# Last product of a pair of experts: one float32 matmul per half tile, or three products of split halves with the weights' halves kept in a table

## What is computed

```python
scores = x @ expert_tokens.T                  # 8 experts, hidden size 64
_, topk_idx = top_k(scores, 2)
for i in range(8):
    w = mean(topk_idx == i)                   # 0.5 for the two chosen experts, else 0
    h = gelu(x @ W1[i] + b1[i])               # [.., 1024] x [1024, 64]
    h = gelu(h @ W2[i] + b2[i])               # [.., 64] x [64, 64]
    y = h @ W3[i] + b3[i]                     # [.., 64] x [64, 1024]
    outputs = outputs + y * w
x = x + outputs                               # x on the right was normalised again for the experts
```

## Time and profile before

| | |
|---|---|
| median of 3 runs | 1637.22 us (1632.99 to 1646.51) |
| the profiled execution | 1640.42 us, its span 1638.7 us |
| mean granted TensorE clock | 0.961 of full |
| busy: TensorE, VectorE, ScalarE, GpSimd | 1489.0, 1193.0, 687.0, 681.2 us |
| moved by DMA | 306.94 MB, 187 GB/s over the span |

### The profile page before, as it was taken

One profiled execution on the slowest core, in us unless ns is written; L12 is line 12 of the kernel. 1 busy time (PEld: TensorE's weight loads), 2 busy tenths in 40 slices (PEclk: granted clock), 3 DMA queues, 4 the chain that ended last, 5 costly groups with the idle time before them and its releaser, 6 DMA issues.

```text
span 1638.7 us, 28903 instructions
## 1 busy us (share of the span) xinstructions
PE 1489.0 (91%) x9321; PEld 1235.5 (75%) x9321; DVE 1193.0 (73%) x2415; ACT 687.0 (42%) x1365; POOL 681.2 (42%) x769
## 2 busy tenths in 40 slices
PE   6999999999699656998989957999999999999997
PEld 5999999999577335877767746777777777777775
DVE  5666666666388675898988974777777777777775
ACT  2444445454243630000000005666566566656653
POOL 2112222223675004677666543444444444444432
PEclk9999999999799887999999978999999999999999
DMA  8888875552564098799999757677677666765420
GB/s 204 227 179 193 174 199 152 163 140 67 133 207 119 1 266 201 208 293 287 264 255 286 211 151 220 211 220 224 213 217 217 208 206 207 218 207 157 120 56 15
DMA packets 121961, 306.94 MB, mean 187 GB/s; under 512 B 64155, under 2 KB 65857, under 8 KB 114315
## 3 DMA queue, kind: packets, MB, share of 16 engines
q1 hardware_dynamic: 60088, 155.40, 34.2%
q0 software_dynamic: 61728, 149.74, 32.6%
HBM read 220.40 MB, written 138.85 MB: 219 GB/s over the span
## 4 chain that ended last, share of the span: by engine, by line
PE 46%; issue 20%; DMA 11%; POOL 9%; DVE 8%; SPq 1%; POOLq 0%; DVEq 0%; ACT 0%
PE psum L1888 14%; DMA agg<-node_table,from_idx 8%; PE psum L1856 7%; PE psum L1564 7%; PE psum L1565 6%; PE psum L1566 6%; PE psum L1886 4%; DVE stat L967 2%; POOL where_from L606 2%; POOL agg L663 2%; DVE cx L1325 2%; POOL xls L639 1%; POOL td L643 1%; POOL rstd L595 1%; PE psum L1744 1%
## 5 line engine op out<-in xcount | busy, mean ns | idle before, releaser
L1888 PE MATMUL psum<-w_raw,gl 128*128 128x512 f32 x528 | 269.2, 591 | 0.0
L911 ACT ACTIVATE xt_hi<-psum 128x512 fp32r<-128x512 f32 x264 | 151.0, 597 | 238.4 <-PE psum L1856 238.3
L1492 DVE TENSOR_TENSOR xt_lo<-psum,xt_hi 128x512 fp32r<-128x512 f32 x264 | 176.3, 688 | 86.3 <-ACT xt_hi L911 86.2
L1603 PE MATMUL psum<-wdx_hi,axt_hi 128*125 128x272 f32 x640 | 191.4, 299 | 6.8 <-DVE wd_lo L1034 4.0
L1505 DVE SCALAR_TENSOR_TENSOR xb<-psum,xb 128x512 f32<-128x512 f32 x264 | 176.0, 686 | 28.0 <-PE psum L1888 27.7
L995 DVE TENSOR_TENSOR axt_lo<-psum,axt_hi 128x500 fp32r<-128x500 f32 x160 | 108.4, 678 | 118.8 <-ACT axt_hi L771 118.8
L1856 PEld LDWEIGHTS psum<-ident,xn 128*128 128x128 f32 x1056 | 126.4, 142 | 86.8 <-issue 68.3
L1605 PE MATMUL psum<-wdx_hi,axt_lo 128*125 128x272 f32 x640 | 185.5, 290 | 0.0
L1604 PE MATMUL psum<-wd_lo,axt_hi 128*125 128x256 f32 x640 | 180.2, 281 | 0.0
L743 POOL DMA_INDIRECT out<-xb,idx_in x132 | 133.8, 1014 | 106.1 <-issue 59.4
L905 ACT ACTIVATE xn<-xb 128x1024 f32<-128x1024 f32 x132 | 156.1, 1233 | 45.1 <-DMA xb<-rows_x,idx_in 45.1
(11 more groups left out here) (277 smaller groups left out, 3872.1 us busy)
## 6 DMA issues: line engine op xcount, KB each, us to landing
w_raw<-in_L_ffn_W SPq DMA_DIRECT2D x140, 256.0 KB, 12.7
cx<-in_x POOLq DMA_DIRECT2D x20, 1792.0 KB, 15.3
rows_x<-cx SPq DMA_DIRECT2D x19, 1806.0 KB
ax<-in_x SPq DMA_DIRECT2D x19, 1792.0 KB
node_table<-trow SPq DMA_DIRECT2D x19, 896.0 KB
node_table<-xld SPq DMA_DIRECT2D x10, 448.0 KB
cx<-in_x POOLq DMA_DIRECT2D x20, 208.0 KB, 23.1
rows_x<-cx SPq DMA_DIRECT2D x19, 209.6 KB
```

Source lines behind the costliest of these rows:

```text
L1492: dve.tensor_tensor(xt_lo[:, 2 * q:2 * q + 2, :].rearrange("p k n -> p (k n)"), T_R[q % 2], xt_hi[:, 2 * q:2 * q + 2, :].rearrange("p k n ...
L1603: pe.matmul(into, high, wdx_hi[:, k, :], start=k == 0, stop=False, skip_group_check=True)
L1888: pe.matmul(Y[u], gl2[:, t % 2, rows], w3_raw[:, t % N3, HALF * n:HALF * (n + 1)], start=False, stop=True, skip_group_check=True).then_inc ...
```

## The change

In the expert tiles `down` multiplies by halves. `gelu_2` is followed by a copy of its result to float32r (`gl2_hi`, ScalarE) and VectorE subtracts (`low_2`, between the next tile's `low_r` and the last two `result`s). The last product becomes three float32r matmuls of 512 columns, and its wait is for the low half instead of the gelu.

The weights' halves come from a new table in DRAM, `w3_parts`, with high and low half side by side in rows of 2,048 numbers. It is made during the projection: SyncE loads all of w3 (2 MB) at group 0, ScalarE and VectorE split a quarter of it in each of groups 2 to 5, and SyncE stores both parts (4 MB) at group 7. As the same room on chip then takes w1, w1's pieces move from groups 1 to 8 to groups 8 to 11, two a group, behind a wait for that store; `w_up` moves from group 9 to 12, and the splitting of w1 to groups 13 to 16, two pieces a group. `load_w3` now brings both halves of a tile's weights, 64 rows of 8 KB for either expert.

Some semaphores are merged to make room for the new ones (the one for the padding with `raw_small`, those for w_up's low halves and for the routing weights into `up_ready`, those for the staged w1 and w2 into `r_w`); the counts that are waited for follow.

```diff
         rows_x1 = nc.dram_tensor("rows_x1", [N, ROW], F32)
+        w3_parts = nc.dram_tensor("w3_parts", [NE * EH, 2 * D], F32)
         lists = nc.dram_tensor("lists", [(PAIRS + 1) * CAP, 1], I32)
...
         tok_rows = put("tok_rows", [NE, D], F32, at1 + 2 * KH * D * 4)
+        w3_low, w3_high, w3_end = run_of(
+            at1 + 2 * KH * D * 4, ("w3_low", [128, NE // 2, D], F32), ("w3_high", [128, NE // 2, D], F32R))
+        assert w3_end <= at2
         before_raw, ones_raw, rest_raw, bcap_i, p_i, b3_hi, b3_raw, late_end = run_of(
...
-        xb, xn0, w3_raw, st_w1, st_w2, r_end = run_of(
+        xb, xn0, w3_hl, st_w1, st_w2, r_end = run_of(
             at3,
-            ("xb", [128, NX, NS, ROW], F32), ("xn0", [128, D], F32), ("w3_raw", [128, N3, D], F32),
+            ("xb", [128, NX, NS, ROW], F32), ("xn0", [128, D], F32), ("w3_hl", [128, N3, 2, D], F32R),
             ("st_w1", [128, 2, 2, KD, 128], F32R), ("st_w2", [128, 2, 2, 128], F32R))
...
         ranks = RK[0:P, 0:J * PAIRS].rearrange("p (j b) -> p j b", j=J)
+        w3_e = w3_parts[:, :].rearrange("(e h) n -> e h n", h=EH)
         x1_g = rows_x1[:, :].rearrange("(g p j) d -> g p (j d)", p=P, j=J)
...
         WP0, WS0 = 0, 4
-        GW1, GS1 = 1, 11
+        GS3, GP3, GW1, GS1 = 2, 7, 8, 13
...
                     load_x(g + NAX)
-                if GW1 <= g < GW1 + KD:
-                    k = g - GW1
-                    sp.dma_start(w1_raw[:, :, 1, k, :],
-                                 w1[:, 128 * k:128 * (k + 1), :].rearrange("e p h -> p e h")).then_inc(raw_w1, 16)
-                if g == GW1 + KD:
+                if g == 0:
+                    sp.wait_ge(tok_tp, 1)
+                    sp.dma_start(w3_low[:, :, :], w3.rearrange("(q a) h n -> (a h) q n", a=2)).then_inc(raw_ffn, 16)
+                if g == GP3:
+                    sp.wait_ge(ffn_lo, NE // 2)
+                    for part, source in ((0, w3_high[:, :, :].bitcast(F32)), (1, w3_low[:, :, :])):
+                        sp.dma_start(w3_parts[:, D * part:D * (part + 1)].rearrange("(q p) n -> p q n", p=2 * EH),
+                                     source).then_inc(w3_put, 16)
+                if GW1 <= g < GW1 + KD // 2:
+                    sp.wait_ge(w3_put, 32)
+                    for k in (2 * (g - GW1), 2 * (g - GW1) + 1):
+                        sp.dma_start(w1_raw[:, :, 1, k, :],
+                                     w1[:, 128 * k:128 * (k + 1), :].rearrange("e p h -> p e h")).then_inc(raw_ffn, 16)
+                if g == GW1 + KD // 2:
                     sp.dma_start(wup_raw[:, :, :], w_up.rearrange("(k p) n -> p k n", p=128)).then_inc(raw_wup, 16)
...
                         wait(sp, w3_in, 32 * t)
-                    sp.dma_start(w3_raw[EH * a:EH * (a + 1), t % N3, :],
-                                 w3[bass.ds(slot + a, 1), :, :].rearrange("e h n -> (e h) n")).then_inc(w3_in, 16)
+                    sp.dma_start(w3_hl[EH * a:EH * (a + 1), t % N3, :, :].rearrange("p v n -> p (v n)").bitcast(F32),
+                                 w3_e[bass.ds(slot + a, 1), :, :].rearrange("e h n -> (e h) n")).then_inc(w3_in, 16)
...
+            def high_w3(q):
+                act.wait_ge(raw_ffn, 16)
+                act.activation(w3_high[:, q, :], w3_low[:, q, :], ACT.Copy).then_inc(ffn_hi, 1)
+
             def high_w1(k):
-                act.wait_ge(raw_w1, 16 * KD)
+                act.wait_ge(raw_ffn, 16 * (1 + KD))
                 hi, _, raw = w1_piece(k)
-                act.activation(hi, raw, ACT.Copy).then_inc(w1_hi, 1)
+                act.activation(hi, raw, ACT.Copy).then_inc(ffn_hi, 1)
...
                     empty_left(i - 1)
-                if i % J == 1 and 0 <= i // J - GS1 < KD:
-                    high_w1(i // J - GS1)
+                if i % J == 1 and 0 <= i // J - GS3 < NE // 2:
+                    high_w3(i // J - GS3)
+                if i % J in (1, 2) and 0 <= i // J - GS1 < KD // 2:
+                    high_w1(2 * (i // J - GS1) + i % J - 1)
                 if i == 0:
...
                 act.activation(gl2[:, t % 2, :], H2[:, 0:TT], ACT.Gelu, bias=b2_of(pair)).then_inc(r_g2, 1)
+                act.wait_ge(r_g2, t + 1)
+                act.activation(gl2_hi[:, t % 2, :], gl2[:, t % 2, :], ACT.Copy).then_inc(r_g2hi, 1)
...
+            def low_w3(q):
+                dve.wait_ge(ffn_hi, q + 1)
+                dve.tensor_tensor(w3_low[:, q, :], w3_low[:, q, :], w3_high[:, q, :].bitcast(F32), ALU.subtract
+                                  ).then_inc(ffn_lo, 1)
+
             def low_w1(k):
                 hi, lo, raw = w1_piece(k)
-                dve.wait_ge(w1_hi, k + 1)
+                dve.wait_ge(ffn_hi, NE // 2 + k + 1)
                 dve.tensor_tensor(lo, raw, hi.bitcast(F32), ALU.subtract)
...
                         late_setup(2 * j + 4)
-                if j == J - 1 and 0 <= g - GS1 < KD:
-                    low_w1(g - GS1)
+                if j == J - 1 and 0 <= g - GS3 < NE // 2:
+                    low_w3(g - GS3)
+                if j >= 2 and 0 <= g - GS1 < KD // 2:
+                    low_w1(2 * (g - GS1) + j - 2)
                 if i == J + 1:
...
+            def low_2(t):
+                dve.wait_ge(r_g2hi, t + 1)
+                dve.tensor_tensor(gl2_lo[:, t % 2, :], gl2[:, t % 2, :], gl2_hi[:, t % 2, :].bitcast(F32), ALU.subtract
+                                  ).then_inc(r_g2lo, 1)
+
             def first_of(t):
...
                     low_r(t + 1, 1)
+                low_2(t)
                 if t >= 1:
...
                 if q == 0:
-                    pe.wait_ge(r_w1, 2 * (t + 1))
+                    pe.wait_ge(r_w, 3 * t + 2)
                     wait(pe, r_g1, t)
...
                     pe.wait_ge(w3_in, 32 * (t + 1))
-                    pe.wait_ge(r_g2, t + 1)
+                    pe.wait_ge(r_g2lo, t + 1)
                 wait(pe, r_res, 4 * (t - 1) + u + 1)
-                rows = slice(128 * s, 128 * (s + 1))
+                rows, cols = slice(128 * s, 128 * (s + 1)), slice(HALF * n, HALF * (n + 1))
                 pe.matmul(Y[u], sel_st[:, t % 2, :], b3_hl[:, HALF * n:HALF * (n + 1)], start=True, stop=False,
                           skip_group_check=True)
-                pe.matmul(Y[u], gl2[:, t % 2, rows], w3_raw[:, t % N3, HALF * n:HALF * (n + 1)], start=False, stop=True,
-                          skip_group_check=True).then_inc(r_y, 1)
+                product(Y[u], (gl2_hi[:, t % 2, rows], gl2_lo[:, t % 2, rows]),
+                        (w3_hl[:, t % N3, 0, cols], w3_hl[:, t % N3, 1, cols]), False, True).then_inc(r_y, 1)
             turn_r(0, 1)
```

More of the change, by code:

```diff
@@ L140, in build @@
             ("steps", [P, J, PAIRS], F32), ("slot_f", [P, J], F32))
-        (gl1, h1_hi, h1_lo, gl2, sel_st, routed_end) = run_of(
+        (gl1, h1_hi, h1_lo, gl2, gl2_hi, gl2_lo, sel_st, routed_end) = run_of(
             0,
             ("gl1", [128, TT], F32), ("h1_hi", [128, TT], F32R), ("h1_lo", [128, TT], F32R),
-            ("gl2", [128, 2, TT], F32), ("sel_st", [128, 2, 128], F32R))
+            ("gl2", [128, 2, TT], F32), ("gl2_hi", [128, 2, TT], F32R), ("gl2_lo", [128, 2, TT], F32R),
+            ("sel_st", [128, 2, 128], F32R))
         xn1, xn_end = run_of(routed_end, ("xn1", [128, D], F32))
@@ L297, in build @@
         r_h2, r_g2, r_y, r_res = sem("r_h2"), sem("r_g2"), sem("r_y"), sem("r_res")
-        r_w1, r_w2, r_sel = sem("r_w1"), sem("r_w2"), sem("r_sel")
+        r_w, r_sel = sem("r_w"), sem("r_sel")
+        r_g2hi, r_g2lo = sem("r_g2hi"), sem("r_g2lo")
         w2_up, w3_in = sem("w2_up"), sem("w3_in")
@@ L629, in _ @@
             pool.wait_ge(setup_v, 9)
-            pool.wait_ge(pad_zero, 16)
+            pool.wait_ge(raw_small, 16 * 8)
             for b in range(NBG):
@@ L1105, in late_setup @@
                 elif k == 6:
-                    dve.wait_ge(b3_split, 1)
+                    dve.wait_ge(setup_v, 11)
                     dve.tensor_scalar(b3_raw[:, :], b3_raw[:, :], dup_rest[:, 0:1], None, ALU.mult
-                                      ).then_inc(b3_split, 1)
+                                      ).then_inc(setup_v, 1)
                 elif k == 7:
-                    dve.wait_ge(b3_split, 2)
+                    dve.wait_ge(setup_v, 12)
                     dve.scalar_tensor_tensor(b3_hl[0:2 * NE, :], b3_hi[:, :].bitcast(F32), dup_mask[:, 0:1],
@@ L1153, in routing_weights @@
                 product = M2[:, 0:KH * NE].rearrange("p (m e) -> p m e", m=KH)
-                dve.tensor_copy(m2[:, :, 0:NE], product).then_inc(m2_split, 1)
-                dve.wait_ge(m2_split, 1)
+                dve.tensor_copy(m2[:, :, 0:NE], product).then_inc(up_ready, 1)
+                dve.wait_ge(up_ready, WP0 + 5 - WS0 + 2)
                 dve.tensor_tensor(m2[:, :, NE:2 * NE], product, m2[:, :, 0:NE].bitcast(F32), ALU.subtract
-                                  ).then_inc(m2_split, 1)
+                                  ).then_inc(up_ready, 1)
             def low_d(c):
```

(4 more changed lines are left out.)

23 lines of the change are left out of this document (11 added, 12 removed).

## The result

The change made the kernel slower: 1672.06 us, the median of four runs (1663.90 to 1687.55), against 1635.11 us for the kernel before (four runs, 1631.67 to 1646.51). The ratio is 1.0203, with a 95% interval of 1.0158 to 1.0247. The forecast was 1601, with a range up to 1624. The profiled execution took 1669.48 us (span 1667.8), 29.1 more in span than the one of before.

What follows compares the result with a forecast made beforehand. TensorE was taken to bound tiles and projection. Terms -43 + 4 + 2 + 1 = -36 us took the profiled 1640.42 to 1604.4, and 3.2 less for the median gave 1601 us; range 1590 to 1624.

Steps and rivals of the forecast that it cites:

- Part 2: Expert tiles' doubled last-weight loads: no cost in loaded tiles (286 GB/s, share 0.93), 4 us at the stage's start.
- -43: Last product in the expert tiles: 0.163 us less a call, 0.65 a tile, 43 us in 264 calls.
- The DMA engines take over: Rival: DMA engines bound the loaded tiles at 274 GB/s, 9.28 us a tile, 1622 us in all; chance 0.15.
- Slower: Rival: DMA engines lose pace in the tiles; at 248 GB/s 10.24 us a tile, +38, 1675 us; chance 0.04.
- the share of 0.9 to 0.95: Sign in the tiles: the DMA engines' share, expected at this level if the forecast held.
- ScalarE's wait for gathered rows: Sign in the tiles: if ScalarE's normalisation waits for gathered rows, the DMA engines are the bound; forecast expected none.
- Tiles over 9.2 us: Sign that the prediction is wrong: expert tiles taking longer than this, where 8.90 us was forecast.
- low_2 and the copy hidden: In the tiles the new VectorE subtraction and ScalarE copy cost nothing, with 0.35 us a tile left on VectorE.
- The start: Start of the tiles: 1 MB more ahead of tile 0's upper w2 on SyncE's queue, taken as 4 us.
- The case of an 8 KB row as two packets: At the tiles' start: split rows would make both loads nearly twice as long beside gathers, up to 12 us more.
- The projection: Making the table in the projection: 2 us for four VectorE subtractions, 1 us for a late table store.
- The late table store: Projection, group 0: w3's 2 MB ahead of the store delays ScalarE's buffer by 0 to 4 us, taken as 1.

Runs made afterwards that it cites:

- e13: Changed kernel with four w3 loads of 32 rows a tile instead of two of 64, each to every other partition within its half: 1686.36 us.
- e14: Changed kernel with four w3 loads of 32 rows a tile instead of two of 64, each to every fourth of all partitions: 1621.50 us.
- e7: Changed kernel with each expert's w3 rows loaded to every other partition instead of one half (product pairs wrong rows): 1597.78 us.
- e2: Changed kernel with w3 loads counted on two semaphores in turn, so two tiles' w3 are in flight: 1685.39 us.
- e11: Changed kernel with the second expert's w3 load on ScalarE's queue, the first's staying on SyncE's: 1689.13 us.
- e15: Changed kernel with four w3 loads of 64 rows of 4 KB a tile, to every other partition (wrong rows): 1634.14 us.
- e1: Changed kernel loading only the high halves of w3 (512 KB a tile), used in place of the low halves too: 1607.09 us.
- e9: Changed kernel with both experts' hidden rows interleaved, so w3 loads to every other partition and the product stays right: 1604.79 us, 0.9773 of the kernel before.
- e10: e9 with w3 loaded behind group 0's table store, its table steps one group later, and tile 0's upper w2 ahead of w3: 1602.42 us, ratio 0.9753.
- e5: Kernel before with the product by halves, but no table: w3 loaded as before and divided in each tile by ScalarE and GpSimd: 1660.69 us.

## Why the prediction was wrong

- **The step that failed** is in Part 2, "Cost taken: nothing": "the engines manage 306 GB/s on this mix", and so 2.54 MB in 8.90 us at a share of 0.93. The added bytes aren't of the mix. They are loads to half the partitions, which take the engines at 229 GB/s (e13 237, against e14's 317). By the row of before that was left unread (243) the added 0.52 MB would have taken 2.2 us of all engines, beside 0.69 x 9.56 = 6.6: 8.8 of 8.90 us, no room left. Measured are 0.94 x 10.01 = 9.4, so 256 / 0.94 = 272 GB/s for a full share in place of 306; with spread loads (e7) it is 276 / 0.84 = 329. In the 0.6 us of a tile that are left the engines aren't all busy; e2 and e11, with more in flight, come to a share of 0.95, and what holds the rest back (SyncE's order, as in e15, or something else) no run separates. The loaded tile became 10.01 instead of 8.95 (e1), in 55 tiles 58 us: -43 turned into +14.5.
- **The rivals.** "The DMA engines take over" had the engine and nearly the price (274 GB/s, measured 272), but took the engines as full to the end: 9.28 us, where the tile lasted 10.01 at a share of 0.94. "Slower", at 248 GB/s and 10.24 us, is nearest in time and in what moved (256 GB/s), and had 0.04: its counterargument, that the projection's small pieces aren't in the tiles, looked at size, not at where a load lands. Of the signs, the share of 0.9 to 0.95 came true in the lost case as well, so it told nothing apart; ScalarE's wait for gathered rows, named for the DMA case, didn't come in 1100 to 1500, GpSimd's wait for lists did. "Tiles over 9.2 us" was the sign that held.
- **Right:** four products 0.93 us a call; a tile of 8.90 (8.95 in e1, TensorE at 400 of 400); low_2 and the copy hidden; the mechanism at the start and its direction.
- **The start**, term +4: two landings of 12.04 and 10.86 us instead of 8.57 and 7.63, TensorE's wait 8.9 instead of 3.2 us. Mis-sized by 2 us. The two landings grew by 6.7 us together, between the 3.4 to 3.8 of the sum's rates and the 16 of doubled landings. The case of an 8 KB row as two packets didn't arise: in the trace of after such a row is one packet of 8,192 bytes.
- **The projection**, terms +2 and +1. The four subtractions cost 0.43 each, 1.7 us: two neighbouring table copies of ScalarE start 5.15 apart there (89.65 and 94.80) instead of 4.72. The mechanism taken from the earlier trace rows is there: the high half of the next product is ready at 92.14, the subtraction of w3 holds its low half back to 92.73, and TensorE waits for the low_h behind it.

```profile
91.60 1.22 DVE L1035 TENSOR_TENSOR w_low<-w_low,w_high 128x1024 f32<-128x1024 f32 x1
92.73 0.67 DVE L1019 TENSOR_TENSOR axt_lo<-psum,axt_hi 128x500 fp32r<-128x500 f32 x1
93.32 0.41 DVE L1024 TENSOR_TENSOR ht_lo<-psum,ht_hi 128x250 fp32r<-128x250 f32 x1
...
93.78 0.39 PE L1601 MATMUL psum<-wl_hi,ht_hi 128*125 128x256 f32 x1 [0.16 <-DVE ht_lo L1024]
```

  The late table store, taken at 1 with a range to 4, cost 6.2 us: at 63.19 the kernel after is 1.75 ahead, at 84.94 it is 4.47 behind. After that wait TensorE's clock was granted at 0.59 from 76 to 80 us, so mostly its lower level of 1.2 GHz. By the same points the same projection lost 8.1 us there in e1 and 1.3 in e7, so 6.2 is the size of one execution; why it varies stays open. The 4 MB store, taken at 0, cost some 0.7.
- Not explained: some 3 us in the edges, where nothing was changed (1 to 3 in e7, e9 and e10 too).

## What to carry to other kernels

Price added bytes by the queue that carries them (its own bytes over its own share), not by the mean over all queues, and look at which partitions a load writes. Here that price would have shown that there was no room, though not the whole loss. A load of 1 MB a tile to one half of the partitions can be a quarter slower than one to all of them, with nothing else in the program different. Where two operands share the partitions, interleave their rows instead of stacking them, and let the layer before write them in that order.

## What the runs showed of the hardware

- Loads of 1 MB a tile to one half of the partitions, all on SyncE's queue with its small loads: 227 to 237 GB/s of full share; spread over all: 294 to 317. A row of 8 KB took 587 ns in the median to a half (after), 309 spread (e7, e14). Row gathers beside them went from 314 (after) to between 354 and 359. At 512 KB a tile the place made no difference (243 and 246).
- Loads to both halves at the same time from two queues were no faster (212 and 273 GB/s). The Trainium skill ("DMA: Bandwidth & Descriptors", section "Issuing engines are not separate DMA queues") states that transfers started by different engines run on the same 16 engines. The trace agrees: with the third queue the share was 0.95 and the pace lower.
- With subtractions of GpSimd between SBUF tiles beside them (1.30 us for 512 columns, e5), VectorE's subtractions of 256 columns between SBUF tiles took 1.38 us or more, all 81 of them in 1100 to 1500, against 0.42 in e7. The three looked at one by one lie over GpSimd's; what makes them longer isn't shown.
